# Two pipelined attentions: key normalisation in other slots, one more query bank, another order on POOL

## What is computed

```python
def _L2_xattn_ref(hidden_states, encoder_hidden_states, attention_mask, Wq, bq, Wk, bk, Wv, bv, Wo, qn_w, kn_w):
    q = (hidden_states @ Wq + bq)          # 16 heads of 128
    k = (encoder_hidden_states @ Wk + bk)  # 4 heads of 128
    v = (encoder_hidden_states @ Wv + bv)
    q = _rmsnorm(q, qn_w); k = _rmsnorm(k, kn_w)
    scores = q k^T / sqrt(128) + attention_mask
    return softmax(scores) v @ Wo

def _L3_xattn_ref(draft_hidden, context_hidden, Wq, Wk, Wv, Wo, q_norm_w, k_norm_w, context_position_ids, draft_position_ids):
    kv_in = concatenate([context_hidden, draft_hidden])  # 64 + 64 keys of each sequence
    q = _rms_norm(q); k = _rms_norm(k); q = _rope(q); k = _rope(k)
    return softmax(q k^T / sqrt(128)) v @ Wo
```

## Time and profile before

| | us |
|---|---|
| median of three runs | 1250.71 (1248.89 to 1251.1) |
| the profiled execution | 1247.73 |
| its span, first to last instruction | 1245.9 |
| PE busy | 1102.2 (88%) |
| DVE busy | 870.7 (70%) |
| ACT busy | 641.6 (51%) |
| POOL busy | 401.9 (32%) |
| stage a2, query group 0 to the last output quarter | 507.92 to 721.1 |
| stage a3, first query turn to the end of the output | 935.21 to 1180.4 |

### The profile page before, as it was taken

How to read it: one execution, slowest core, us unless ns; L and a number is a source line. 1 busy time by engine, 2 the same in 40 slices (tenths; PEclk the granted TensorE clock), 3 DMA queues, 4 the chain that set the end, 5 groups by cost and what they waited for, 6 DMA issues and landing times.

```text
span 1245.9 us, 21217 instructions
## 1 busy us (share of the span) xinstructions
PE 1102.2 (88%) x7123; PEld 735.4 (59%) x7123; DVE 870.7 (70%) x1954; ACT 641.6 (51%) x1500; POOL 401.9 (32%) x376
## 2 busy tenths in 40 slices
PE   4876878999958999888999988999987999999986
PEld 3554654444445665456767755777643667777844
DVE  7789976888857673567667477544496888886566
ACT  5665544677724322465554343222365767777353
POOL 0050002222203002122222125777526565556123
PEclk9757977999978999988999979999999999999989
DMA  8010017000023224300000074533472000000011
GB/s 269 2 35 11 1 41 315 1 2 1 2 85 124 73 85 161 112 0 1 1 2 1 1 268 152 211 123 103 131 277 68 9 20 25 18 10 9 10 42 34
DMA packets 46102, 88.25 MB, mean 71 GB/s; under 512 B 9073, under 2 KB 32369, under 8 KB 44209
## 3 DMA queue, kind: packets, MB, share of 16 engines
q1 hardware_dynamic: 40720, 72.52, 16.3%
q0 software_dynamic: 5280, 14.42, 3.7%
HBM read 68.84 MB, written 20.05 MB: 71 GB/s over the span
## 4 chain that ended last, share of the span: by engine, by line
PE 62%; DVE 22%; issue 6%; ACT 4%; DMA 3%; POOL 2%; SPq 1%; DVEq 0%; ACTq 0%; POOLq 0%; PEldq 0%
PE psum L2578 5%; PE psum L2125 4%; PE psum L3194 4%; PE psum L2142 3%; PE psum L2598 3%; PE psum L3175 3%; PE psum L1698 2%; PE psum L1274 2%; PE psum L2079 2%; PE psum L3554 2%; PE psum L3144 2%; PE psum L3164 2%; PE psum L2057 2%; PE psum L1716 2%; PE psum L3121 2%
## 5 line engine op out<-in xcount | busy, mean ns | idle before, releaser
L1469 DVE TENSOR_REDUCE c_max<-psum 128x2 f32<-128x512 f32 x128 | 84.2, 680 | 17.0 <-PE psum L1274 15.1
L1369 ACT ACTIVATE c_probs<-psum 128x512 f32<-128x512 f32 x128 | 75.1, 597 | 32.8 <-PE psum L1285 32.6
L3295 ACT ACTIVATE a_probs<-psum,a_max,a_q_rstd 128x128 f32<-128x128 f32 x128 | 56.9, 458 | 17.5 <-DVE a_max L3345 17.3
L2578 PE MATMUL psum<-m_experts,m_tileT 128*128 x188 | 63.7, 461 | 1.6 <-DVE m_tileT L2815 1.6
L3194 PE MATMUL psum<-a_wo,a_outT 128*128 128x256 f32 x256 | 60.1, 379 | 0.7 <-DVE x_tok L3402 0.7
L2655 ACT ACTIVATE m_tile_silu<-psum 128x176 f32<-128x176 f32 x47 | 14.9, 318 | 82.1 <-PE psum L2578 82.1
L1698 PE MATMUL psum<-m_w,m_tileT 128*128 x120 | 54.5, 597 | 3.0 <-DVE m_tileT L1888 3.0
L2215 ACT ACTIVATE a_probs<-a_probs,a_max 128x64 f32<-128x64 f32 x128 | 42.7, 334 | 24.0 <-DVE a_max L2275 24.0
L2887 POOL DMA_INDIRECT m_back<-m_out_tiles,m_rows_of_slots x47 | 46.7, 994 | 19.0 <-issue 11.3
L3194 PEld LDWEIGHTS psum<-a_wo,a_outT 128*128 128x128 f32 x256 | 47.3, 190 | 9.3 <-issue 3.7
L1274 PE MATMUL psum<-c_qk_stacked 32*128 32x256 bf16 x256 | 49.1, 283 | 1.4 <-ACT c_qk_stacked L1357 1.3
(11 more groups left out here) (587 smaller groups left out, 3272.1 us busy)
## 6 DMA issues: line engine op xcount, KB each, us to landing
m_w<-m_w SPq DMA_DIRECT2D x8, 1536.0 KB, 14.7
m_experts<-m_e SPq DMA_DIRECT2D x16, 608.0 KB, 12.1
a_wq<-a_wq SPq DMA_DIRECT2D x2, 2048.0 KB, 10.4
m_rows_back<-m_back SPq DMA_DIRECT2D x4, 1024.0 KB, 9.0
a_ctx_kv<-a_ctx_k_v SPq DMA_DIRECT2D x8, 512.0 KB, 4.0
ctxT_yT_hi<-f_gate_up SPq DMA_DIRECT2D x2, 1024.0 KB, 7.4
...
```

Source lines behind the costliest of these rows:

```text
L1369: e.activation(c1P[:, n % 8, :, :], ps[:, 2 + n % 2, :].rearrange("p (k t) -> p k t", k=2), ACT.Exp, scale=float(1.0 / np.sqrt(np.float32( ...
L1469: e.tensor_reduce(c1M[:, u % 2, j, :], ps[:, c1_score_bank(n), :].rearrange("p (q t) -> p q t", q=2), AX.X, ALU.max).then_inc(c1_mx, 1)
L2578: ins = e.matmul(ps[:, 4 + t % 2, 0:M2_UP], m2xT[:, t % 2, kc, :], m2e[:, bass.ds(own + kc * M2_UP, M2_UP)], start=(kc == 0), stop=(kc == ...
L3295: ins = e.activation(a3sc[:, u % 3, p_ * P:(p_ + 1) * P], ps[:, u % 2, p_ * P:(p_ + 1) * P], ACT.Exp, bias=a3mx[:, u % 3, p_:p_ + 1], scal ...
```

## The change

1. a2, key steps. `keys_biased` goes from lag 4 to 7, `key_squares` from 3 to 5, `key_sums` and POOL's power from 3 to 4; `keys_normed` stays at lag 3, the turn at 1. One step of a pair's keys now stands in each of the slots `4i - 7`, `4i - 5`, `4i - 4`, `4i - 3`, `4i - 1`.
2. a2, query squares. `squares_reduced(g)` leaves the end of slot `g - 6` for the slot after, behind that slot's query bias.
3. a2, PE and DVE. Groups 0 to 6 alternate between banks 6 and 7 and wait for the bias of the group before the last. Bank 7 is the output's, which is first written in slot 7.
4. a3, POOL only. Power and normalisation of a batch's keys go from lag 5 to 4. In a slot the rotation comes ahead of the normalisation and ahead of the roots of the query sums.

No instruction is added or left out on any engine.

```diff
+        def a2_q_bank(g):
+
+            return 7 if g < A2_AHEAD and g % 2 else 6
@@ a2_pe, queries
-                if g:
-                    e.wait_ge(*a2_qb.at(g))
+                lead = 1 if g < A2_AHEAD else 0
+                if g > lead:
+                    e.wait_ge(*a2_qb.at(g - lead))
...
-                    ins = e.matmul(ps[:, 6, :], ...
+                    ins = e.matmul(ps[:, a2_q_bank(g), :], ...
@@ a2_act
-                if a2_pair(n, 3) is not None:
-                    key_squares(a2_pair(n, 3))
+                if a2_pair(n, 5) is not None:
+                    key_squares(a2_pair(n, 5))
@@ a2_dve
+                if a2_group(n, 2 - A2_AHEAD) is not None:
+                    squares_reduced(n + A2_AHEAD - 2)
...
-                if a2_pair(n, 3) is not None:
-                    key_sums(a2_pair(n, 3))
+                if a2_pair(n, 4) is not None:
+                    key_sums(a2_pair(n, 4))
...
-                if a2_pair(n, 4) is not None:
-                    keys_biased(a2_pair(n, 4))
-                if a2_group(n, 1 - A2_AHEAD) is not None:
-                    squares_reduced(n + A2_AHEAD - 1)
+                if a2_pair(n, 7) is not None:
+                    keys_biased(a2_pair(n, 7))
@@ a2_pool
-                if a2_pair(n, 3) is not None:
-                    i = a2_pair(n, 3)
+                if a2_pair(n, 4) is not None:
+                    i = a2_pair(n, 4)
@@ a3_pool
-                if a3_batch(n, 5) is not None:
-                    b = a3_batch(n, 5)
+                if a3_batch(n, 4) is not None:
+                    b = a3_batch(n, 4)
                     ...
                     e.tensor_tensor(a3rk[:, b % 2, :], ..., ALU.pow).then_inc(a3_rk.sem, 1)
+                if a3_unit(n, 1 - A3_AHEAD) is not None:
+                    queries_rotated(n + A3_AHEAD - 1)
+                if a3_batch(n, 4) is not None:
+                    keys_normed(a3_batch(n, 4))
                 if a3_pair(n, 1) is not None:
                     ...
                     e.tensor_tensor(a3rq[:, i % 2, :], ..., ALU.pow).then_inc(a3_rq.sem, 1)
-                if a3_batch(n, 5) is not None:
-                    keys_normed(a3_batch(n, 5))
-                if a3_unit(n, 1 - A3_AHEAD) is not None:
-                    queries_rotated(n + A3_AHEAD - 1)
```

4 lines of the change are left out of this document (2 added, 2 removed).

## The result

The changed kernel took 1230.13 us (median of four runs, 1229.22 to 1230.83), the kernel before 1249.8 (four runs, 1245.61 to 1251.1: the three known before and one more). The ratio is 0.984, with a 95% interval of 0.9821 to 0.9859: 19.7 us saved. The forecast was 1233.5. The profiled execution took 1230.08 us, its span is 1228.3 (before 1245.9), the mean granted clock 0.925.

The account below looks back on a forecast made before the run. PE was taken to wait only in the attention starts, for DVE's key chain (a2) and ACT's query copy (a3). Savings 13.8 + 2.0 + 6.4 = 22.2 us, less 5.0 for clock falls, gave 17.2: 1233.5 us, range 1228 to 1241.5.

Parts of the forecast that it names:

- First slots of a2: a2 slots -7 to 0: query group 7 comes at 524.7 instead of 531.05 us, 6.4 us saved.
- Slots 1 to 7: a2, query group 7 to group 14: 33.4 us instead of 40.8, with short PE gaps left.
- The 13.8 us: a2 start: saving by query group 14, from 21 us of waits, restarts and half clock less 7.2 remaining.
- Tail of a2: a2, scores 14 and the output products behind: the 1.06 us wait and 1.8 us go, 2.0 us taken as saved.
- a3: Start of the fourth attention: POOL's new order brings the fifth query turn sooner, 6.4 us saved in all.
- The wait at the key turn: a3 start: a new PE wait of 1.9 us for POOL's normalisation at the key turn of batch 1.
- the stop before the fifth turn: a3 start: PE's stop before the fifth query turn shrinks from 5.92 to 2.0 us.
- The clock: Both attention starts: PE may fall to 1.2 GHz behind new gaps; two falls put back, 5.0 us (bounds 0 and 9).
- The port: a3: POOL's power beside DVE's key products does not hold DVE, nothing charged; as a rival 1238.5 us, 10%.
- Rival, ACT takes DVE's place: a2: ACT becomes the bound, slots 1 to 7 win nothing, 9.0 us saved in all, 1241.7 us; 20%.
- Rival, key turns wait all along: a3: with 1.1 us to spare, 13 key turns each wait 1.9 us for POOL, 25 us lost, 1258 us; 4%.

Follow-up runs that it names:

- x2_spread: Kernel before with only the a2 key steps spread (bias lag 7, squares 5, sums and power 4), one query bank; 1264.56 us, ratio 0.9911 to before.
- x6_squares_behind: Changed kernel, but in a2 ACT squares the keys behind the probability and key copies instead of ahead; 1253.24 us, ratio 0.9804 to the kernel before.
- x10_norm_twice: Changed kernel with POOL's normalisation of the keys done twice in a3; 1259.61 us, ratio 0.9886 to the kernel before.
- x0_after: The changed kernel itself, run again on another chip; 1256.35 us, ratio 0.9835 to the kernel before on that chip.
- x4_a3: Kernel before with only POOL's new order in a3 (part 4 of the change); 1270.71 us, ratio 0.9951 to the kernel before.
- x5_norm_first: Changed kernel, but in a3 POOL normalises the keys ahead of the slot's rotation instead of behind; 1257.77 us, ratio 0.9831 to the kernel before.
- x7_keys_early: Changed kernel with PE's key turn and ACT's key copy one slot earlier in a2 (lag 2 instead of 1); 1253.21 us, ratio 0.9791 to the kernel before.

## Why the prediction was right, point by point

- **First slots of a2** (group 7 at 16.7 us behind group 0, 6.4 saved): 16.91, 6.2 saved. The order replay was right. By the runs about 2.5 of it is the key steps (x2_spread) and 3.7 the bank on top of them.
- **Slots 1 to 7** (33.4 us): 33.16, with 1.66 of half clock in it. Named and sized right: 1.4 at group 8 (1.26), 2.6 before scores 2 (2.27) with 0.5 of it the change's own (x6_squares_behind: 0.52). Wrong: 0.4 and 1.8 us before groups 10 and 13; the first was 0.17, the second did not come here, and was 0.69 in x10_norm_twice, which has the same a2 without a fall. The 13.8 us were counted at full clock and 13.87 came with a fall among them that cost 0.7 us at group 14 (see below), so the gaps had been summed 0.8 too long. That 13.8 and 13.87 agree is luck: a gap too long and a fall not in this term offset each other.
- **Tail of a2** (2.0): 2.9. I had counted less than the two rows gave, 1.06 and 1.8, for no reason in a row.
- **a3** (6.4 before the clock): 5.7 in x0_after, 5.5 in x4_a3, 4.2 with the stretch of half clock in the first profile. The wait at the key turn was 1.73 against 1.9 forecast, the stop before the fifth turn 1.69 against 2.0. x5_norm_first shows that the first of these costs nothing: it is taken from the second.
- **The clock** (two falls put back, 5.0): two came, one in each attention, but only one behind a stop that the forecast had named, the 2.27 us before scores 2. The other, at 962.50 in a3, stands behind stops of 0.94 and 0.84 us that it had not, while at its 1.73 and 1.69 us the clock stayed up, and x0_after does without it. So the count of two is partly luck. The price was too high. From scores 2 to the next turn of probabilities it was 5.66 us in the changed kernel (545.05 to 550.71) and 4.00 in x6_squares_behind, which stayed at full clock (543.94 to 547.94): 1.66 on the spot. But without the fall DVE's next stop, before group 13, comes instead, and at group 14 only 0.7 is left (50.07 against 49.37 us in x10_norm_twice). In a3, turn 14 came at 95.48 us with the fall behind 962.50 and at 93.97 in x0_after without it: 1.51. So the term was 2.2 and not 5.0; I had taken 2 to 2.7 for each from the old rows. The forecast's list of falls also lacks one: the clock fell near the first query turn of a3, behind 2.79 us, before (from 936.63) and after (from 921.93). The second turn stands 14.7 us behind the first product in both, so nothing of the saving hangs on it.
- **The port** (charged nothing): right, as the row at 940.97 shows.
- **Rival, ACT takes DVE's place**: ACT's key copy is indeed the next bound, but its stop is 2.27 us in all, not the 7.7 us that slots 1 to 7 won. x7_keys_early shows that it is an order that can be changed.
- **Rival, key turns wait all along**: the spare time was 2.78 us and not 1.1. The step that failed is that I took DVE's products and PE's turn at their old distance, 3.45 us; DVE now has them done 5 us ahead of the turn. In the long stretch before it waited 6.7 us for POOL's roots and 6.5 for its rotations, and both waits are gone. The rival's worry was right for the start of the stage, where the key turn of batch 3 had 0.36 us to spare.

As a whole: I summed 17.2, and the two attentions gave 21.0 in the first pair of profiles. The 3.8 between are 0.8 (gaps of slots 1 to 7), 0.9 (tail), 2.8 (clock), less 0.7 (a3). Of the 21.0, 3.4 went into stages that the change does not touch, most of it lost in c1 ahead of a2; that the spans differ by 17.6, so close to 17.2, is luck. The saving by the medians, 19.7, lies between. Where the waits stand and who ends them was right on the whole; the term that was mis-sized most is the clock's.
